# Attention block: scores transposed (keys on the partitions), row sums from one f32 product, division after P·V

## The reference, cut to what matters

```
q = rms_norm(x @ wq);  k = rms_norm(x @ wk);  v = x @ wv        # 16 heads; 4 kv heads
k_ctx = rms_norm(ctx @ wk_ctx);  v_ctx = ctx @ wv_ctx
q, k = rope(q), rope(k)
k_full, v_full = concat([k_ctx, k]), concat([v_ctx, v])         # 512 keys
scores = q @ k_full.T / sqrt(128), causal on the own keys
out = softmax(scores) @ v_full @ wo
```

## Time and profile before

| what | value |
|---|---|
| median of 3 runs | 1545.94 us (1544.02 to 1547.71) |
| the profiled execution | 1547.26 us, its span 1546.0 us |
| PE busy / weight loads | 1488.8 us (96%) / 1165.6 us (75%) |
| DVE, ACT, POOL busy | 1137.2 us (74%), 959.3 us (62%), 692.1 us (45%) |
| granted TensorE clock, mean | 0.993 |
| last store of the attention's output | issued at 876 us |

### The profile page before, as it was taken

The page is one execution under the profiler, slowest core; times in us unless marked ns, Lnnn a source line. Parts: engine busy times, 40 slices in busy tenths (PEclk is TensorE's granted clock), DMA queues, the critical chain, the costliest instruction groups (busy, mean ns, idle before and its releaser), DMA issues. The chain is left out here.

```text
span 1546.0 us, 26210 instructions
## 1 busy us (share of the span) xinstructions
PE 1488.8 (96%) x8644; PEld 1165.6 (75%) x8644; DVE 1137.2 (74%) x2966; ACT 959.3 (62%) x2470; POOL 692.1 (45%) x832
## 2 busy tenths in 40 slices
PE   7899999999999999999999999999998899999988
PEld 6778888888888888888888666666666566666653
DVE  6787677777776877777788765555566898888774
ACT  5666666666666656666667765555546577666655
POOL 4564555464645555555567300000015455555544
PEclk9999999999999999999999999999999999999999
DMA  7011111111111111111144789778866301111000
GB/s 281 28 42 55 42 69 42 42 69 42 56 56 42 69 42 42 69 42 56 57 190 177 263 288 292 260 248 261 260 210 203 99 9 54 56 49 42 28 14 28
DMA packets 84327, 165.09 MB, mean 107 GB/s; under 512 B 39392, under 2 KB 39520, under 8 KB 82784
## 3 DMA queue, kind: packets, MB, share of 16 engines
q1 hardware_dynamic: 84192, 163.41, 30.8%
HBM read 113.05 MB, written 41.94 MB: 100 GB/s over the span
## 5 line engine op out<-in xcount | busy, mean ns | idle before, releaser
L617 ACT ACTIVATE Pt<-Pt,small 128x384 f32<-128x384 f32 (+1 forms) x256 | 172.7, 682 | 106.1 <-DVE small L877 106.0
L368 PE MATMUL bank<-wq,xT 128*128 128x512 f32 x768 | 206.7, 404 | 1.0 <-DVE wq L772 1.0
L421 PE MATMUL bank<-PT,vv 128*128 128x512 f32 x672 | 199.6, 405 | 4.7 <-DVE PT L862 3.8
L1135 POOL TENSOR_SCALAR Pt<-Pt,small 128x384 f32<-128x384 f32 (+1 forms) x256 | 164.0, 653 | 79.0 <-DVE small L885 78.9
L877 DVE CUSTOM_DVE_ANT_0 Pt<-quad,mask,small 128x384 f32<-128x384 f32 (+1 forms) x256 | 171.6, 679 | 30.7 <-PE quad L398 29.4
L1356 PE MATMUL bank<-wq,ot 128*128 128x512 f32 x768 | 182.1, 395 | 1.5 <-DMA ot<-ot_scratch 1.5
L862 DVE TENSOR_TENSOR PT<-quad,PT 128x512 fp32r<-128x512 f32 x224 | 153.6, 686 | 37.9 <-ACT PT L609 37.5
L1356 PEld LDWEIGHTS bank<-wq,ot 128*128 128x128 f32 x768 | 143.9, 188 | 33.7 <-DMA ot<-ot_scratch 2.2
L368 PEld LDWEIGHTS bank<-wq,xT 128*128 128x128 f32 x768 | 136.8, 189 | 26.4 <-DVE wq L772 2.3
L1123 POOL TENSOR_TENSOR t<-t 128x512 f32<-128x512 f32 x64 | 83.6, 1306 | 144.1 <-DVE t L843 144.1
L421 PEld LDWEIGHTS bank<-PT,vv 128*128 128x128 f32 x672 | 116.4, 189 | 28.9 <-DVE PT L862 10.2
(11 more groups left out here) (286 smaller groups left out, 3502.6 us busy)
## 6 DMA issues: line engine op xcount, KB each, us to landing
ot_scratch<-OT SPq DMA_DIRECT2D x64, 512.0 KB, 2.9
ot<-ot_scratch SPq DMA_DIRECT2D x64, 512.0 KB, 5.7
wkv_f<-in_w SPq DMA_DIRECT2D x12, 512.0 KB, 6.5
wkc_f<-in_w SPq DMA_DIRECT2D x12, 512.0 KB, 6.9
wkv_f<-in_wg SPq DMA_DIRECT2D x11, 512.0 KB, 6.9
wkv_f<-in_wd SPq DMA_DIRECT2D x11, 512.0 KB, 6.6
wkv_f<-in_wu SPq DMA_DIRECT2D x10, 512.0 KB, 7.1
stg<-in_ctxT SPq DMA_DIRECT2D x16, 256.0 KB, 4.1
```

The lines of the kernel that those rows point to most:

```text
L368: ins = pe.matmul(bQ[:], xT[p][:, k, qt * 128:qt * 128 + 128], wq[j][:, g, k, :], start=(part == 0 and k == 0), stop=(part == 2 and k == 3))
L421: ins = pe.matmul(bO[:], vv[x][:, bg % 2, kt, :], PT[y][:, k % 2, :], start=(kt == 0 and n == 0), stop=(kt == tiles_in(i) - 1 and n == 2))
L617: act.activation(p, p, ACT.Exp, bias=nm[:, i % 2, h:h + 1], scale=-1.0, accum_out=sm[:, i % 2, h:h + 1]).then_inc(f["s_exp"], 1)
L1135: pool.tensor_scalar(p, p, ri[:, i % 2, h:h + 1], 1.0, ALU.mult, ALU.mult).then_inc(f["p_n"], 1)
```

## The change

Scores are made with the **keys on the partitions**: for each tile c of 128 keys one product over all four heads, `quad[:, c, :]` 128 keys x 512 (4 heads x 128 queries). The result is already P's transpose, so `pe_p_turn` goes. What was done per query row must be done another way:

- the query's norm multiplies the rotated query ahead of its transposition (`act_q_n`, four ACT copies with a scale, in t1);
- the own key's norm, a value per partition now, is the exponential's scale (`act_exp`, part 1); own keys are roped unnormed (`dve_k_n` copies them); context keys are normed as before;
- the row's minimum goes; a fixed shift, `min(60 - sqrt(128)*max|qw|*max|kw|, 0)`, is made once (`dve_shift`);
- the causal mask is a product of POOL with a 0/1 triangle on the exponentiated tile (`pool_mask`);
- P is split straight from SBUF into PT (tiles 0 and 1 in one instruction of 128x1024; `act_p_hi`, `pool_p_hi`, `dve_p_lo`);
- row sums: POOL adds tiles 0 and 1 (`pool_t_pair`), DVE adds the rest (`dve_t_sum`), `pe_sum` multiplies the sum tile by an f32 matrix of ones, DVE turns the result in 32x32 squares, inverts 128x16 values and turns them back (`dve_s_turn`, `dve_ri`);
- the output is multiplied by the inverse as it leaves PSUM (`dve_o`), then split by ACT (`act_o_hi`) and POOL (`pool_o_lo`, in place).

The norms of queries and keys are taken together (`dve_ve`, `pool_norms`: up to 6 columns). All hand-written orders are new; `pe_keep` (bf16 filler products in blocks 63 and 64) goes; the x tiles of SP are issued ahead of a block's store instead of behind it, the mask's DMA shrinks from 128x512 to 128x128 and waits for `x_first` on SP.

```diff
-    def pe_s(i, h):
+    def pe_s(i, part):
...
+        after(pe, f["s_exp"], 2 * i - 1 + part)
...
+        for c in chunks(i, part):
+            for n, (x, y) in enumerate(PRODUCTS):
+                ins = pe.matmul(quad[:, c, :], kT[x][:, bg % 2, c * 128:c * 128 + 128], qT[y][:],
+                                start=(n == 0), stop=(n == 2))
+        ins.then_inc(f["s_mm"], 1)
-    def pe_p_turn(i, kt):
...
+    def pe_pv(i, part):
...
+        pe.wait_ge(f["pt_lo"], 2 * i + part + 1)
+        if part == 0:
...
+            after(pe, f["o_split"], 2 * i - 1)
+    def pe_sum(i):
+
+        pe.wait_ge(f["t_add"], 2 * i + 2)
+        pe.wait_ge(f["qt_lo"], min(i + 2, NBLK))
...
+        pe.matmul(bT[:], ones[:], tt[:], start=True, stop=True).then_inc(f["sum_mm"], 1)
+    def pe_odd(i):
+        pe_kv(i + 2)
+        pe_s(i, 0)
...
+        pe_sum(i - 1)
+        pe_q(i + 2, 0)
+        pe_pv(i - 1, 0)
+        pe_pv(i - 1, 1)
+        pe_k_turn(i + 2)
+        pe_s(i, 1)
+        pe_q(i + 2, 1)
+        pe_q(i + 2, 2)
+        pe_q_turn(i + 1)
...
     def pe_even(i):
...
+        pe_kv(i + 2)
...
+        pe_s(i, 0)
...
+        pe_pv(i - 1, 0)
...
+        pe_sum(i - 1)
+        pe_s(i, 1)
+        for part in range(3):
+            pe_q(i + 2, part)
+        pe_k_turn(i + 2)
+        pe_q_turn(i + 1)
+        pe_pv(i - 1, 1)
+    def act_q_n(i):
...
+        act.wait_ge(f["norms"], q_normed(i))
+        act.wait_ge(f["q_rot"], 2 * i + 1)
+        for h in range(4):
+            t = t1[:, h * 128:h * 128 + 128]
+            ins = act.activation(t, t, ACT.Copy, scale=q_norm(i)[:, h:h + 1])
...
+        c = chunks(i, part)
+        if part == 0:
+            ins = act.activation(P[:, 0:2, :], quad[:, 0:2, :], ACT.Exp, bias=shift)
+        else:
...
+            for t in range(1 + i % 2):
+                ins = act.activation(P[:, 2 + t, :], quad[:, 2 + t, :], ACT.Exp, bias=shift, scale=k_norm(u)[:, t:t + 1])
...
+    def act_p_hi(i, own=0):
...
+        act.copy(PT[0][:, s, :], P[:, s, :]).then_inc(f["p_hi"], 1)
+    def dve_p_lo(i, part):
...
+        hi, lo = (w[:, c[0]:c[-1] + 1, :] for w in PT)
+        dve.tensor_tensor(lo, P[:, c[0]:c[-1] + 1, :], hi.bitcast(F32), ALU.subtract).then_inc(f["pt_lo"], 1)
+    def dve_t_sum(i):
...
+        if i % 2:
+            v.did(dve.tensor_tensor(t, t, P[:, 2, :], ALU.add))
+            v.settle()
+        dve.tensor_tensor(t, t, P[:, 2 + i % 2, :], ALU.add).then_inc(f["t_add"], 1)
+    def dve_s_turn(i):
...
+        dve.transpose(sT[:], bT[:]).then_inc(f["s_ri"], 1)
+    def dve_ri(i):
...
+        v.did(dve.reciprocal(rsum, sT[:].rearrange("p (c n) -> p c n", n=32)[:, :, 0]))
+        v.settle()
+        v.did(dve.transpose(ri[:].rearrange("p (c n) -> p c n", n=32), rsum.unsqueeze(2).broadcast_to((128, 16, 32))))
+    def dve_o(i):
...
+        dve.wait_ge(f["pv_mm"], 2 * i + 2)
+        after(dve, f["ot0"], 16 * i)
+        v.settle()
+        dve.tensor_tensor(OT[:, 1, :].bitcast(F32), bO[:], ri[:], ALU.mult).then_inc(f["o_split"], 1)
+    def dve_odd(i):
...
+        dve_q(i + 1)
+        dve_q_lo(i)
...
+        dve_t_sum(i - 1)
+        dve_k_n(i + 2)
+        if i > 1:
+            dve_p_lo(i - 1, 0)
+        dve_o(i - 2)
+        dve_ve(i)
+        dve_p_lo(i - 1, 1)
+        dve_v_lo(i + 2)
...
+        dve_s_turn(i - 1)
+        dve_p_lo(i, 0)
+        dve_k_lo(i + 2)
+        dve_ri(i - 1)
...
     def dve_even(i):
...
+        dve_q(i + 1)
+        dve_q_lo(i)
...
+        dve_o(i - 2)
+        dve_t_sum(i - 1)
...
+    def pool_odd(i):
+        pool_q_add(i + 1)
+        pool_k_rope(i + 2)
+        pool_norms(i)
...
+        pool_t_pair(i)
+        pool_o_lo(i - 2)
+        pool_mask(i)
...
     def pool_even(i):
         pool_q_add(i + 1)
...
+        pool_p_hi(i - 1)
+        pool_norms(i)
+        pool_t_pair(i)
+        pool_mask(i)
+        pool_o_lo(i - 2)
+        pool_p_hi(i)
```

More of the change, by code:

```diff
@@ L169, in x_bank, with q_norm, k_norm, q_normed @@
     def x_bank(m):
-        return bQ if m % 2 else bT
+        return quad[:, 3, :] if m % 2 else bT[:]
     def xb4(m):
-        return x_bank(m)[:].rearrange("p (k n) -> p k n", k=4)
+        return x_bank(m).rearrange("p (k n) -> p k n", k=4)
+    def q_norm(j):
+        return norms[:, (j - 1) % 4, 0:4]
+    def k_norm(u):
+        return norms[:, (u - 2) % 4, 4:6]
+    def q_normed(j):
+        return j + 3 if j else 2
+    def k_normed(u):
+        return u + 2 if u > 1 else 2 * u + 1
+    def sums(m, part=None):
+        first, last = 0 if m + 1 < NBLK else 4, 6 if m + 2 < NU else 4
+        if m < 0:
+            first, last = (0, 4) if part == "q" else (4, 6)
+        return first, last
+    def summed(m, part=None):
+        return m + 4 if m >= 0 else 1 if m == -2 else 2 if part == "q" else 3
+    def hi_made(i, own=0):
+        return i + i // 2 + 1 + own
     def keys(u):
@@ L381, in pe_q_turn @@
         ins.then_inc(f["qt_mm"], 1)
-    def pe_s(i, h):
+    def pe_s(i, part):
         if i >= NBLK:
             return
-        bg, n = i // 2, width(i)
-        bank = bS[h % 2]
-        if h == 0:
+        bg = i // 2
+        if part == 0:
             pe.wait_ge(f["kt_lo"], 2 * bg + 2)
             pe.wait_ge(f["qt_lo"], i + 1)
-        if i == 61 and h == 1:
+        if i == 61 and part == 1:
             pe.wait_ge(f["w_gamma"], 1)
-        after(pe, f["s_ev"], 4 * i + h - 1)
-        qh, ql = (qT[j][:, h * 128:h * 128 + 128] for j in range(2))
-        kh, kl = (kT[j][:, bg % 2, 0:n] for j in range(2))
-        pe.matmul(bank[:, 0:n], qh, kh, start=True, stop=False)
-        pe.matmul(bank[:, 0:n], ql, kh, start=False, stop=False)
-        pe.matmul(bank[:, 0:n], qh, kl, start=False, stop=True).then_inc(f["s_mm"], 1)
@@ new lines, in pe_s @@
+        if part:
+            pe.wait_ge(f["xt_lo"], min(2 * ((i + 1) // 8) + 2, NT))
+        for c in chunks(i, part):
[4 more added lines that the diff above has]
+    def pe_pv(i, part):
+        if i < 0:
+            return
+        bg = i // 2
+        pe.wait_ge(f["pt_lo"], 2 * i + part + 1)
+        if part == 0:
+            pe.wait_ge(f["v_lo"], max(2 * bg + 2, 3))
+            pe.wait_ge(f["kt_lo"], max(2 * bg + 2, 3))
+            after(pe, f["o_split"], 2 * i - 1)
+        last = chunks(i, 1)[-1]
+        for c in chunks(i, part):
+            for n, (x, y) in enumerate(PRODUCTS):
+                ins = pe.matmul(bO[:], vv[x][:, bg % 2, c, :], PT[y][:, c, :],
+                                start=(c == 0 and n == 0), stop=(c == last and n == 2))
+        ins.then_inc(f["pv_mm"], 1)
@@ L794, in dve_x_lo, with dve_ve @@
         dve.tensor_tensor(xT[1][:, :, sl], xb4(m), xT[0][:, :, sl].bitcast(F32), ALU.subtract).then_inc(f["xt_lo"], 1)
-    def dve_k_ss(u):
-        if u >= NU:
+    def dve_ve(m, part=None):
+        if m + 1 >= NBLK:
             return
-        dve.wait_ge(f["k_sq"], u + 1)
-        dve.tensor_scalar(kve[:, 0:2], kss[:, 0:2], 128e-6, None, ALU.add).then_inc(f["k_ve"], 1)
+        first, last = sums(m, part)
+        if first == 0:
+            dve.wait_ge(f["q_sq"], m + 2)
+        if last == 6:
+            dve.wait_ge(f["k_sq"], m + 3)
+        after(dve, f["norms"], summed(m, part) - 1)
+        dve.tensor_scalar(sve[:, first:last], ss[:, first:last], 128e-6, None, ALU.add).then_inc(f["sums_ve"], 1)
     def dve_k_n(u):
@@ new lines, in dve_o, with dve_shift @@
+    def dve_o(i):
+        if i < 0:
+            return
+        dve.wait_ge(f["pv_mm"], 2 * i + 2)
+        after(dve, f["ot0"], 16 * i)
+        v.settle()
+        dve.tensor_tensor(OT[:, 1, :].bitcast(F32), bO[:], ri[:], ALU.mult).then_inc(f["o_split"], 1)
+    def dve_shift():
+        for w, top in ((4, qw_max), (6, kw_max)):
+            v.did(dve.tensor_reduce(top, rope[:, w, :], AX, ALU.max, apply_absolute_value=True))
+        v.settle()
+        v.did(dve.scalar_tensor_tensor(bound, qw_max, -ROOT, kw_max, ALU.mult, ALU.mult))
+        v.settle()
+        dve.tensor_scalar(shift, bound, EXP_ROOM, 0.0, ALU.add, ALU.min).then_inc(f["tables"], 1)
@@ L1100, in pool_ln_rs, with pool_norms @@
         pool.tensor_tensor(rs[:, t:t + 1], ve[:, t:t + 1], half[:, 0:1], ALU.pow).then_inc(f["ln_rs"], 1)
-    def pool_k_rs(u):
-        if u >= NU:
+    def pool_norms(m, part=None):
+        if m + 1 >= NBLK:
             return
-        pool.wait_ge(f["k_ve"], u + 1)
-        pool.tensor_tensor(krs[:, 0:2], kve[:, 0:2], half[:, 0:2], ALU.pow).then_inc(f["k_rs"], 1)
+        first, last = sums(m, part)
+        pool.wait_ge(f["sums_ve"], summed(m, part))
+        after(pool, f["s_exp"], 2 * m)
+        pool.tensor_tensor(norms[:, m % 4, first:last], sve[:, first:last],
+                           half[:, 0:1].broadcast_to((128, last - first)), ALU.pow).then_inc(f["norms"], 1)
     def pool_k_rope(u):
```

682 lines of the change are left out of this document (252 added, 430 removed).

## The result

The change made the kernel **slower by half a per cent**: 1554.6 us, median of 4 runs (1553.45 to 1556.07), against 1546.8 us of the kernel before on the same chip; the ratio is 1.0053, its 95% interval 1.0035 to 1.0071. The forecast was 1515 us. The profiled execution took 1556.1 us, its span 1554.7, so 8.7 us more span than before.

The account below looks back on a forecast made before the run. PE's own list was taken as the bound: a pair 26.04 - 2.7 + 1.6 = 24.94 us, so -35 over 32 pairs, +4 at the ends, -31 in all: 1515 us. Own range 1490 to 1539; with rivals 1482 to 1568.

Parts of the forecast that it names:

- P's transpositions: PE in mid-attention: seven groups of four products go from each pair of blocks, 0.39 us each, -2.7 us a pair.
- the f32 product: PE's `pe_sum`, one product of 512 columns a block: taken at 0.8 us, +1.6 us a pair (0.9 to 1.8).
- third rival: PE gains more: f32 product costs 0.46 (22 us less), fewer stops give 0.3 a pair; 1484 us, chance 0.12.
- the high bound: PE's f32 product: two instructions, each at half the fp32r rate, 4 x 0.23 = 0.92 us.
- POOL's load: POOL's work in a pair: 17.4 us, with port collisions 22.2 of PE's 24.9; it fits, but barely.
- the port: Port shared by DVE and POOL: if each DVE operation from SBUF collides, POOL gets 4.8 us a pair longer.
- Rival 1: Port and POOL become the bound: 25.8 to 27.4 us a pair, slower, middle 1576 us; chance 0.25.
- The waits of the middle: Added waits through POOL and OT's store against fewer PE waits: counted as nothing, 0.5 us a pair (16 us) kept for range.
- The ends: Prologue +3 us, end of attention +1 together with a looser last block: sum +4 us.
- the x tiles' DMAs ... so nothing: SP's list: x tiles ahead of one store in eight blocks cost nothing, as their `c_lo` precedes that store's `o_lo`.
- The bf16 fillers that went ran in idle time: End of attention: removing PE's filler products was given no cost of its own.
- the query's 3 us: Prologue: first query transposition must wait for squares, norm and `act_q_n`, 1.0 + 0.15 + 1.02 + 0.8 = 3 us.

Follow-up runs that it names:

- the doubled one: Changed kernel with the f32 product of the row sums made twice: 1596.7 us, one run.
- the repaired kernel: Changed kernel with the last blocks' lists reordered: 1530.0 us; with bf16 fillers back, 1528.4; with ACT's second weight conversions also moved up, 1524.3.
- no addition: Changed kernel with POOL's addition of tiles 0 and 1 cut to a single column: 1546.0 us, one run.
- the cheaper copy: Changed kernel with POOL's p_hi copy written with two operations in place of one: 1542.8 us, one run.
- the last kernel: Changed kernel with repaired tail, fillers, ACT's prologue weights moved up and POOL's two-operation copy: 1513.3 us, ratio 0.9783 to the kernel before.

## Why the prediction was wrong, point by point

**PE, right in kind, a little low in size.** P's transpositions went, the f32 product costs 0.86 us where 0.8 was taken. By the prediction's price of the transpositions the pair should then be 2.7 - 1.7 = 1.0 us shorter; an ordinary one is 1.57 shorter. The larger part of the 0.6 beyond is a misreading of the transpositions. The prediction took 0.35 us from a group of four to the next start. PE's timeline before shows where more of the price is, in the product behind the group:

```profile
412.15 0.48 PE L396 MATMUL quad<-kT,qT 128*128 128x512 f32 x1
412.47 0.39 PE L397 MATMUL quad<-kT,qT 128*128 128x512 f32 x1
```

That product has 0.32 us to the next start where its like have 0.23 (411.34 to 411.57 in the earlier trace rows). So a group costs 0.35 + 0.09 = 0.44, as the other group, 0.43, said by itself, and seven groups cost 3.0 to 3.1 and not 2.7. 3.05 - 1.72 = 1.3; the other 0.25 or so may be the third rival's "fewer stops", and was not taken apart. The third rival's other half (0.46 for the f32 product) is refuted, though the records seem to show it: from the product's first start to the next product's start are 0.45 us. What they hide is seen in the product behind them: 433.62 to 434.96 is 1.34 us for four products that otherwise take 0.91 (4 x 0.23). PE's timeline after:

```profile
433.17 1.02 PE L449 MATMUL bank<-tt,ones 128*128 128x512 f32 x2
433.62 1.50 PE L393 MATMUL bank<-wq,xT 128*128 128x512 f32 x4
434.96 2.23 PE L439 MATMUL bank<-PT,vv 128*128 128x512 f32 x9
```

(With 0.45 + 0.43 the product costs 0.88, close to the 0.86 of the doubled one.) Either lies between the 0.8 that was taken and the high bound of 0.92.

**POOL's load: sum right, terms wrong.** The forecast had 22.2 us of 24.9, 89%; the window shows 89.27%. Two errors met: the copies were priced at 0.70 each from L1135 in the earlier trace rows, a two-operation form, and took 1.51 (+1.6 a pair); the port was taken at 4.8 us a pair, where additions (+1.1), powers (+0.9) and rope (+1.2) together came out some 3.2 above the prices taken for them. That the sum came out at 89% is luck. The copies stand ahead of P·V of the own keys, and the longer form of them cost 11.8 us in one run, 11.0 in the repaired kernel. This is the first mis-sized term: two copies a pair at 0.70.

**The port: there, but not a bound.** POOL's big additions took 1.29 to 1.65 us, DVE's splits of 128x1024 from SBUF 1.31. Rival 1 put the limit at 25.8 to 27.4 us a pair; the ordinary pair stayed at 23.97 with PE 98% busy, and neither more load on the port nor less on POOL moved it; the eighth-block pair they did move, by +0.2 and -0.6. That the kernel came out slower, as this rival said, is no success of it: the middle became faster, and the loss stands at the ends, where the rival had the forecast's 4 us. A DVE split that was already running cost a power that came behind it 0.90 us; a DVE product that came behind a power was not delayed; a DVE addition that came behind POOL's context split was, by 1.0 us. The Trainium skill, "SBUF — State Buffer", section "SBUF: two separate sides", says that the one that starts first has the shared ports for its whole instruction and the other is blocked. The first observation agrees with it (0.90 of the 1.04 left) and so does the third; the second does not, and for a power on POOL the measurement decides.

**The waits of the middle: right at ordinary pairs, missed at the eighth-block ones.** Waits of PE from 203 to 745 us, which answer to the earlier trace rows:

```profile
PE bank L375 <- POOL kk L1082: 6.0, 6, 1.0
PE bank L439 <- DVE OT L892: 4.3, 13, 0.5
```

10 us in all, where "0.5 us a pair" had been kept for the range. The extras of an eighth block cost 3.3 us a pair where they cost 2.0 before. POOL's load has its part in that: with less on POOL they cost 2.7 (no addition) and 2.5 (the cheaper copy), and POOL's context splits come on top of a POOL that is 89% full; the forecast added their time to POOL's average over all pairs (0.65), but they fall on one pair in four.

**The ends: this is the step that failed.** The prediction counted "Prologue ... 3 us. End: ... I take +1 together with a looser last block. Sum +4". With the four pairs on either side it came to -4.8; measured +37.5. The single sentence "the x tiles' DMAs ... so nothing" looked at SP's list for the one step that was moved. It did not ask what else stands behind a store whose releaser had moved: `o_lo` went from DVE to a late place in POOL's list, and w1, wo and w2 stand behind that store (16.2 us in the whole when they were moved up, 10.6 of them between the marks of the last blocks). ACT's conversion of wo, moved ahead of all the exponentials of an odd block, then held them and `act_q_n`. POOL's last piece of wo stood behind `o_lo(63)` (8.0 us). "The bf16 fillers that went ran in idle time" held for PE's time; put back in the repaired kernel, they were worth 1.6 us by the clock, at most. In the prologue the query's 3 us were priced rightly (PE waits 2.7 us for the first `act_q_n`) and are part of the 4.3; ACT's second piece of weights, for which PE waited, was worth 4.1 us and stood in no term.

**What stays open.** With everything repaired the last blocks still take 146.4 us against 136.7 before, where 3.4 less were forecast. PE is idle 12.7 of the last 61 us, where it was idle 3.5 of 46 before; its longest waits there are 3.0 us for the FFN's first input from DVE, 2.2 for P's low part and 2.0 for the next query. The window of the last kernel:

```profile
794.00:855.00 61.00, 48.28 (x203) 32.82 (x202) 48.02 (x68) 38.80 (x65) 36.42 (x26) 0.97 0.55 194
```

In blocks without projections for later blocks there is less to lay beside the longer way from scores to output; that this is the reason is argued, not shown, and so is whether it can be shortened.

## What to carry to other kernels

When a step moves to another engine or another place in its list, look beyond its readers: list what stands **behind each instruction that waits for it**, on SP too, in the blocks where that list holds something else than usual. A schedule in steady state says nothing of the first and last iterations; give them a sum of their own, with a chain and a fill, and measure them as stretches of their own. When a change with good arithmetic loses, cut the span at marks that both kernels have before the arithmetic is doubted.
